# A second buffer of masked B*C products, made in step 5, and an earlier second tap, in a fused Mamba-2 and expert kernel

## What is computed

```python
gate, xBC, dt = split(hidden @ in_proj_w.T)
xBC = silu(conv(xBC, conv_w, 4 taps, causal) + conv_b)
x, B, C = split(xBC)                   # x: 128 heads of 64, B and C: 8 groups of 128
cs = cumsum(dt * A)                    # per head, inside a chunk of 128
L = exp(cs[l] - cs[s]) for s <= l, else 0
scores = (C @ B.T) * L
y = scores @ (x * dt) + (what came from the chunk before) + x * D
y = groupwise_rmsnorm(y * silu(gate)) * norm_w
out = y @ out_proj_w.T
```

## Time and profile before

| | |
|---|---|
| median of 3 runs | 1792.17 us (1789.79 to 1793.70) |
| profiled execution | 1795.43 us, span 1793.3 us |
| TensorE busy (matmul) | 1689.9 us, 94% |
| VectorE busy | 1470.5 us, 82% |
| ScalarE busy | 1025.0 us, 57% |
| GpSimd busy | 926.5 us, 52% |
| mean granted TensorE clock | 0.979 |

### The profile page before, as it was taken

The page is one execution under the profiler, slowest core; times in us unless marked ns, Lnnn a source line. Parts: engine busy times, 40 slices in busy tenths (PEclk is TensorE's granted clock), DMA queues, the critical chain, the costliest instruction groups (busy, mean ns, idle before and its releaser), DMA issues.

```text
span 1793.3 us, 31306 instructions
## 1 busy us (share of the span) xinstructions
PE 1689.9 (94%) x9236; PEld 1318.9 (74%) x9236; DVE 1470.5 (82%) x1729; ACT 1025.0 (57%) x1601; POOL 926.5 (52%) x593
## 2 busy tenths in 40 slices
PE   7699989999899998999899989999899989999997
PEld 5477867777677776777677767777677767777775
DVE  6534697888789798989799898978898888979886
ACT  4223566666466655666566656665566656666551
POOL 3432265565465554555465555555465545555552
PEclk9799999999999999999999999999999999999999
DMA  3321222212221222112212221112121222212203
GB/s 116 118 82 67 84 80 64 62 56 65 66 68 51 63 69 63 60 53 72 65 57 56 67 71 55 59 57 74 56 69 47 72 63 63 62 54 76 67 20 141
DMA packets 73458, 121.39 MB, mean 68 GB/s; under 512 B 12366, under 2 KB 17870, under 8 KB 73252
## 3 DMA queue, kind: packets, MB, share of 16 engines
q1 hardware_dynamic: 72676, 117.92, 21.9%
q10 hardware_dynamic: 576, 1.05, 0.2%
HBM read 112.64 MB, written 6.29 MB: 66 GB/s over the span
## 4 chain that ended last, share of the span: by engine, by line
PE 69%; DVE 17%; issue 9%; ACT 3%; POOL 1%; DMA 1%; DVEq 0%; ACTq 0%; SPq 0%; POOLq 0%
PE pj L455 12%; PE pj L457 12%; PE pj L456 12%; PE ob L455 6%; PE sc L622 5%; PE ob L456 5%; PE ob L457 5%; DVE conv L1222 4%; DVE decay L1250 3%; PE seg L601 3%; PE tb L611 2%; PE sc L626 2%; DVE acc L1304 2%; DVE wo_lo L1286 2%; DVE xc L1236 1%
## 5 line engine op out<-in xcount | busy, mean ns | idle before, releaser
L959 POOL TENSOR_TENSOR w_lo<-stg,w_hi 128x512 fp32r<-128x512 f32 x316 | 501.6, 1588 | 510.2 <-ACT w_hi L827 413.5
L455 PE MATMUL pj<-xT_hi,w_hi 128*128 128x512 f32 x1208 | 488.5, 404 | 31.8 <-DVE conv L1222 28.2
L457 PE MATMUL pj<-xT_hi,w_lo 128*128 128x512 f32 x1208 | 478.6, 396 | 0.0
L456 PE MATMUL pj<-xT_lo,w_hi 128*128 128x512 f32 x1208 | 478.3, 396 | 0.0
L1222 DVE SCALAR_TENSOR_TENSOR conv<-pj,par,conv 128x510 f32<-128x510 f32 (+2 forms) x480 | 357.1, 744 | 42.2 <-ACT conv L835 30.8
L989 POOL TENSOR_TENSOR xc<-xc,thg 128x512 f32<-128x512 f32 x128 | 209.5, 1636 | 227.0 <-DVE xc L1273 227.0
L455 PEld LDWEIGHTS pj<-xT_hi,w_hi 128*128 128x128 f32 x1208 | 230.9, 191 | 95.6 <-DVE conv L1222 28.7
L1250 DVE TENSOR_TENSOR decay<-decay,gm 128x1536 f32<-128x1536 f32 x128 | 285.8, 2233 | 0.0
L457 PEld LDWEIGHTS pj<-xT_hi,w_lo 128*128 128x128 f32 x1208 | 231.2, 191 | 50.6
L456 PEld LDWEIGHTS pj<-xT_lo,w_hi 128*128 128x128 f32 x1208 | 231.3, 191 | 45.9
L455 PE MATMUL ob<-wo_hi,yT_hi 128*128 128x512 f32 x540 | 224.0, 415 | 7.0 <-DVE part L1299 4.4
(11 more groups left out here) (169 smaller groups left out, 2307.0 us busy)
## 6 DMA issues: line engine op xcount, KB each, us to landing
stg<-wstream SPq DMA_DIRECT2D x387, 256.0 KB, 2.6
rowt<-cs_scr SPq DMA_DIRECT2D x384, 4.0 KB
colt<-cs_scr SPq DMA_DIRECT2D x384, 4.0 KB
acc<-hid SPq DMA_DIRECT2D x8, 256.0 KB, 4.4
decay<-gate_scr SPq DMA_DIRECT2D x8, 256.0 KB, 4.4
xc<-hid SPq DMA_DIRECT2D x8, 256.0 KB, 5.2
out<-acc SPq DMA_DIRECT2D x8, 256.0 KB, 2.0
gate_scr<-part SPq DMA_DIRECT2D x4, 256.0 KB, 2.0
```

Source lines behind the costliest of these rows:

```text
L455: nc.tensor.matmul(dst, hi_w, hi_x, start=first, stop=False)
L456: nc.tensor.matmul(dst, hi_w, lo_x, start=False, stop=False)
L457: return nc.tensor.matmul(dst, lo_w, hi_x, start=False, stop=last)
L959: nc.gpsimd.tensor_tensor(w_dest(n, 1), stg[:, s % RING, :], f32(w_dest(n, 0)), ALU.subtract).then_inc(S["wl"], 1)
```

## The change

- `gm` gets a buffer for each half.
- TensorE: the B*C products of the following half move from the end of step 5 to just behind its x block, ahead of the transposes. They wait for pair 6's exponential instead of pair 7's.
- TensorE: the exponents of pair 7 move from behind the scan of step 5 to behind its out-projection. They now wait for the mask products (except in the last half).
- ScalarE: in step 5 the decays (of pair 7) come after the tanh of the x block instead of before it.
- VectorE: the mask products move from step 6 to step 5, from behind the weighting to behind the taps. They wait for the last weighting of the half before the current one, as that is the last reader of this buffer.
- VectorE: in steps 4 and 6 the taps of the second x block move up to behind the adding of the scan; its silu stays last.
- The router's small tiles, which lay in `gm` before the groups begin, lie in its second buffer.

```diff
-        gm = sb("gm", [P, 2, 3 * P])
+        gm = sb("gm", [P, 2, 2, 3 * P])
...
-            def bc_products(g, half, n):
+            def bc_products(g, half):
                 pe.wait_ge(S["silu"], at(g, half, NX, 2))
-                pe.wait_ge(S["exp"], at(g, half, NJ, n))
+                pe.wait_ge(S["exp"], at(g, half, NJ, -1))
...
             def exponents(g, half, n):
+
+                if n == NJ - 1 and not is_last(g, half):
+                    pe.wait_ge(S["gm"], at(g, half, 2, 4))
                 if n == 0:
                     pe.wait_ge(S["gm"], at(g, half, 2, 2))
...
                 if mine:
                     channel_block(g, half, mine[0])
+                if s == 5 and not is_last(g, half):
+                    bc_products(*following(g, half))
                 if has_pair(g, half, s + 1):
                     x_turn(*pair(g, half, s + 1))
                 if has_pair(g, half, s):
                     scan(g, half, s)
-                if has_pair(g, half, s + 2):
+                if s != 5 and has_pair(g, half, s + 2):
                     exponents(*pair(g, half, s + 2))
                 if len(mine) > 1:
                     channel_block(g, half, mine[1])
                 if with_out:
                     out_of_step(g, half, s)
-                if s == 5 and not is_last(g, half):
-                    bc_products(*following(g, half), 0)
+                if s == 5 and has_pair(g, half, s + 2):
+                    exponents(*pair(g, half, s + 2))
...
-                if has_pair(g, half, s + 2):
+                if s != 5 and has_pair(g, half, s + 2):
                     decays(*pair(g, half, s + 2))
                 if mine:
                     x_tanh(*of_half(g, half, mine[0][1]), mine[0][1])
+                if s == 5 and has_pair(g, half, s + 2):
+                    decays(*pair(g, half, s + 2))
...
             def mask_products(g, half):
                 dve.wait_ge(S["bcp"], at(g, half, 1, 1))
-                dve.wait_ge(S["w"], at(g, half, NJ, 0))
+                dve.wait_ge(S["w"], at(g, half, NJ, -NJ))
                 for b in range(2):
-                    nc.vector.tensor_tensor(gm[:, b, :], seg[:, b, 0:3 * P], tri3, ALU.mult).then_inc(S["gm"], 1)
+                    nc.vector.tensor_tensor(gm[:, half, b, :], seg[:, b, 0:3 * P], tri3, ALU.mult).then_inc(S["gm"], 1)
...
-                if s == 6 and not is_last(g, half):
-                    mask_products(*following(g, half))
                 if mine:
                     taps(g, half, mine[0])
+                if s == 5 and not is_last(g, half):
+                    mask_products(*following(g, half))
                 if has_pair(g, half, s + 1):
                     x_times_dt(*pair(g, half, s + 1))
                 if has_pair(g, half, s):
                     add_scan(g, half, s)
+                for m in mine[1:]:
+                    taps(g, half, m)
...
                 for m in mine[1:]:
-                    taps(g, half, m)
                     x_silu(*of_half(g, half, m), m)
```

More of the change, by code:

```diff
@@ L297, in build @@
         wT_lo = [wo_hi[0:NE, 7, :], wo_lo[0:NE, 7, :]]
-        rt = gm[:, :, :].rearrange("p a b -> p (a b)")
+        rt = gm[:, 1].rearrange("p a b -> p (a b)")
         le = rt[:, 0:128].rearrange("p (t e) -> p t e", t=NTT)
@@ L1249, in block_weights @@
                 d = decay[:, n % NDEC].rearrange("p (b h) c -> p b h c", b=2)
-                nc.vector.tensor_tensor(d, d, gm[:, :, :].unsqueeze(2).to_broadcast([P, 2, 2, 3 * P]), ALU.mult
+                nc.vector.tensor_tensor(d, d, gm[:, half].unsqueeze(2).to_broadcast([P, 2, 2, 3 * P]), ALU.mult
                                         ).then_inc(S["w"], 1)
```

## The result

The changed kernel takes 1733.72 us (median of 4 runs, 1732.07 to 1734.05) against 1792.30 us (median of 4). The ratio is 0.9674, 95% interval 0.9660 to 0.9688: 58.6 us or 3.3% faster. The forecast was 1760.7 us, with a range of 1744 to 1786: the direction is right, and the gain is nearly twice the 31.5 us worked out.

The account below looks back on a forecast made before the run. TensorE, busy 94%, was near the matmul rate, with VectorE deciding its first-half pauses. Groups 1 to 6 gain 26.4 us, group 0 4.6, group 7 3.0, second halves lose 2.5: 31.5 us, giving 1760.7 us; range 1744 to 1786.

Parts of the forecast that it names:

- Where the time is lost: All of TensorE's loss lies in first halves; 4.4 us gained per half, 26.4 us over groups 1 to 6.
- First link, the taps of step 4: Step 4, first halves: earlier taps of x1 cut VectorE's idle from 3.69 to about 0.4 us; 2.9 us kept as gain.
- Masks in step 5: Two mask products, 1.02 us together, move from step 6 to step 5: zero in sum, their wait for the silu covered.
- The new pause at step 5's end: TensorE waits about 0.9 us for the mask products before pair 7's exponents in first halves; this hides.
- ScalarE's late high part: Step 5: out weights' high part ready near 667.1 where VectorE asks for it at 666.7: 0.4 us lost.
- The loop end on VectorE (2.46 us) stays.: First halves, ahead of the gate of step 7: VectorE's 2.46 us at its loop's end remain after the change.
- rival (b): TensorE becomes the only bound: its idle and slow stretch go, about 10.5 us per half, 1719 to 1744 us; chance 0.03.
- the slow stretches: TensorE's pauses partly move to the next steps; 0.7 us per half charged for a new stretch at low clock.
- VectorE's neighbour: VectorE operations beside GpSimd grow: 1.4 us charged in step 6; as a rival, 1770 to 1782 us, chance 0.22.
- Second halves: Masks end about when the out-projection does: 0 to 0.7 us lost each, 7 x 0.35 = 2.5 us.

Follow-up runs that it names:

- The experiment on the kernel before: The kernel before with only the cut of VectorE's loop moved, to step 1 of a second half: 1788.24 us, ratio 0.9978.
- the own wait and the cut moved: Changed kernel, VectorE waiting for its own last silu ending step 6 of first halves, its loop cut at step 1 of second halves: 1731.77 us.

## Why the prediction was right in direction and wrong in size

From one mean square of step 1 to the next, group 2's first half (first line) and the second half behind it, before:

```profile
607.50:715.20 107.70, 99.98 (x547) 77.58 (x545) 93.88 (x100) 63.90 (x101) 54.59 (x34) 0.97 0.23 65
715.20:806.80 91.60, 91.37 (x526) 72.42 (x527) 79.21 (x94) 56.96 (x89) 53.95 (x34) 1.00 0.19 58
```

and after:

```profile
597.00:694.50 97.50, 96.44 (x546) 75.68 (x544) 92.37 (x98) 63.94 (x100) 54.93 (x34) 1.00 0.24 71
694.50:786.40 91.90, 91.66 (x526) 72.52 (x527) 81.63 (x94) 57.13 (x89) 53.58 (x34) 1.00 0.20 58
```

- **Where the time is lost: right.** Nearly all the gain is in first halves. This one is 10.2 us shorter. The first halves of groups 1 to 6 took 106.4 to 107.9 us each before and take 97.5 to 98.0 now, 55.8 us less together, where I had 26.4.
- **First link, the taps of step 4: right** as a link, and shown by the run with only those taps late (28.8 us). That the gate of step 5 came out to 0.2 us is luck. I had ScalarE's loop end at 2.21 us and no wait for the gate's tanh; ScalarE stood 3.15 us and VectorE 1.09. So 2.1 us of idle went instead of 3.3, and VectorE's operations got 1.0 us shorter where I had them 0.4 longer.
- **Masks in step 5: right as a sum** (1.01 us, the wait for the silu of x1 covered), except in group 0. There the B*C products wait 2.37 us for this silu, and a slow block follows (265.50 in the timeline). Group 0's first half gained 1.4 us, not the 4.6 I gave it. Group 7 has such a wait too (1.14 us); its first half gained 3.1 us where I had 3.
- **The new pause at step 5's end: right.** 0.61 us at 652.32, forecast 0.9.
- **ScalarE's late high part, 0.4 us: right.** VectorE idles 0.38 us for it at 656.12.
- **The step that failed: "The loop end on VectorE (2.46 us) stays."** I took a duration of the trace as a property of the place. It depends on what stands ahead: the silu of x4 waited 0.89 us for a tanh, and only then did the loop end begin. Without that wait it runs beside instructions already handed to VectorE. Exposed again, it costs 14.4 us, 2.4 per half. With it fell my objection to rival (b), TensorE as the only bound, to which I gave 0.03. The measured time lies inside that rival's range (1719 to 1744) and outside my forecast, and its mechanism is what the trace shows: 10.2 us went per half where it had 10.5, and TensorE idles for 0.8 to 1.4 us in each first half of groups 1 to 7.
- **Mis-sized: the slow stretches.** I charged 0.7 us per half for pauses moved to the next steps. They did not come: the list has 5.1 us of waits before projection blocks in the whole kernel, and 1.00 as the clock of the stretches above.
- **Mis-sized: VectorE's neighbour.** By the gates of steps 6 and 7, VectorE was 1.2 and another 1.1 us ahead of my sum, apart from the loop end. The silus of x grew (median 1.77 us, 1.29 before; mean 1.42, 1.29 before), but the low part of the out weights in step 5 and the output sum of step 6 took 0.75 and 0.74 us, where they took 1.78 and 1.77 before. Over the kernel the low part of y, which I had not counted, grew most, by 22.3 us in all, the silus of x by 17.4, and others became shorter. Before and after:

```profile
L1278 DVE TENSOR_TENSOR yT_lo<-xc,yT_hi 128x512 fp32r<-128x512 f32 x128 | 88.5, 691 | 1.8 <-ACT yT_hi L864 1.8
L1285 DVE TENSOR_TENSOR yT_lo<-xc,yT_hi 128x512 fp32r<-128x512 f32 x128 | 110.8, 866 | 1.9 <-ACT yT_hi L869 1.9
```

  The rule on the shared port pair that the prediction names (the Trainium skill, SBUF — State Buffer, "SBUF: two separate sides") agrees with the trace on which operations grow: these have two inputs in SBUF, while the gate's silu, which reads a bank, stays at 0.68 us in both kernels. That VectorE's lead at these two gates comes from this was read from one half and not tested by a run.
- Per half: 4.4 forecast, plus 2.46 for the loop end, 2.3 for the neighbour, 0.7 for the clock, is 9.9, against 9.3 on average. Only the first of the three has a run of its own.
- **Second halves: nearly right.** 0.4 us lost in all, where I had 2.5.
- The experiment on the kernel before shows the other half of the lesson: the same 2.46 us were worth 3.8 us there and 14.4 us in the changed kernel. I missed it in the expectation of that run too, by looking at VectorE's gaps and not at TensorE's.

## What to carry to other kernels

Look at what a late instruction in an in-order queue releases on the *other* engines. Moving the three taps of a block ahead of four other instructions, in two steps of eight, gave 48 of 58 us, while the larger-looking part of the change gave 10. Put a loop's end where the engine has work in its queue, not behind a wait; and when a wait ahead of it is removed, ask whether the loop end goes with it. A new wait on the bound engine needs its cover named: the same wait, one out-projection earlier, cost the whole gain. With a second buffer, move the producer only as far as the consumer needs.

## What the runs showed of the hardware that I had not expected

- A loop end leaves VectorE idle for 2.4 to 3.3 us and ScalarE for 2.0 to 3.4 us where the engine had just waited, and VectorE for nothing visible where it is still executing: 15 to 19 us in 6 times on VectorE in one case, no such entry in its waits in the other, from the same loop. The transfers of instructions agree with this. In the changed kernel one of 8 KB starts between 669.1 and 670.8, while VectorE executes the low part ahead of its loop end, and one more before the gate of step 7. In the kernel before, one starts between 691.2 and 693.6, when VectorE stands idle. The line of this queue in the idle stretch of before, and from 669.1 to 670.8 in the changed kernel (transfers, MB, share of 16 engines):

```profile
q14 instruction: 1, 0.01, 1.0%
q14 instruction: 1, 0.01, 1.3%
```

  With the own wait and the cut moved, this queue has none from 668 to 674 us, and one from 691 to 693.6. That these transfers are VectorE's is concluded from their moving with its cut. The Trainium skill (Runtime: NRT & Kernel Launch, "Instruction fetch mechanics") says that a taken branch breaks the sequential fetch of instructions, and that the engine must wait for a transfer where the target is not among the two pages at hand. That fits; no run here tells the time of the transfer from that of the branch itself.
- A pause of 2.39 us can halve TensorE's clock, or not. In the run with the exponents at their old place, second halves have this same pause at the same step. Of the seven, 2.37 to 2.39 us long, four are followed by a stretch at the lower clock and three are not. The stretches behind it in group 2 and in group 4 (columns as above):

```profile
763.40:768.90 5.50, 5.50 (x29) 4.44 (x27) 3.75 (x5) 3.10 (x4) 3.07 (x2) 1.00 0.09 10
...
1157.40:1162.90 5.50, 5.50 (x19) 4.38 (x18) 3.49 (x4) 3.09 (x4) 3.04 (x2) 0.69 0.12 19
```

  The first stays at 2.4 GHz, the second is partly at 1.2. Which pause is followed by a slow stretch was not settled here.
